# Attention scores of a head pair as two 64-row matmuls instead of stacked 128-row ones

## What is computed

```python
q  = (ln @ Wq).reshape(b, m, h, d).transpose(0, 2, 1, 3)
kv = concatenate([xn @ Wkv, ln @ Wkv], axis=1)        # context rows and token rows
qn = rmsnorm(q, qn_g) * d ** -0.5
kn = rmsnorm(k, kn_g)
sim  = einsum('bhid,bhjd->bhij', qn, kn)              # the scores
attn = softmax(sim, axis=-1)
out  = einsum('bhij,bhjd->bhid', attn, v) @ Wout + bout
```

## Time and profile before

| what | value |
|---|---|
| runs of the kernel before | 2625.65, 2631.70, 2632.07 us |
| span of the profiled execution | 2631.3 us, on its one core |
| mean granted TensorE clock over the span | 0.981 of full |
| TensorE matmuls busy | 2504.6 us, 95% of the span |
| TensorE weight loads busy | 2050.5 us, 78% |
| VectorE, ScalarE, GpSimd busy | 1856.0, 1692.0 and 1309.6 us |
| first and last score matmul start | 93.9 and 1804.3 us |

### The profile page before, as it was taken

One profiled execution on the slowest core, in us unless ns is written; L12 is line 12 of the kernel. 1 busy time (PEld: TensorE's weight loads), 2 busy tenths in 40 slices (PEclk: granted clock), 3 DMA queues, 4 the chain that ended last, 5 costly groups with the idle time before them and its releaser, 6 DMA issues. The chain is left out here.

```text
span 2631.3 us, 45112 instructions
## 1 busy us (share of the span) xinstructions
PE 2504.6 (95%) x14568; PEld 2050.5 (78%) x14568; DVE 1856.0 (71%) x2516; ACT 1692.0 (64%) x2286; POOL 1309.6 (50%) x783
## 2 busy tenths in 40 slices
PE   3799999999999999999999999987989999999998
PEld 3677777777777777777777777755989999999997
DVE  7677777777767767777777776765876557676775
ACT  2578777777777877777777777764332334444443
POOL 4445544454445444554445444531543526666665
PEclk8899999999999999999999999998999999999999
DMA  5845565556646565456645665564841449999996
GB/s 187 242 129 143 166 164 150 134 165 168 167 126 170 150 171 144 134 166 166 156 134 162 167 163 134 134 163 99 174 111 59 139 156 320 322 318 320 326 320 175
DMA packets 258066, 466.63 MB, mean 177 GB/s; under 512 B 65704, under 2 KB 145884, under 8 KB 254025
## 3 DMA queue, kind: packets, MB, share of 16 engines
q1 hardware_dynamic: 231318, 406.54, 54.9%
q0 software_dynamic: 25696, 58.82, 8.3%
q10 hardware_dynamic: 978, 0.34, 0.1%
HBM read 280.90 MB, written 79.85 MB: 137 GB/s over the span
## 5 line engine op out<-in xcount | busy, mean ns | idle before, releaser
L726 DVE TENSOR_TENSOR pr_lo<-pr,pr_hi 128x1024 fp32r<-128x1024 f32 x576 | 816.9, 1427 | 380.8 <-ACT pr_hi L840 376.3
L839 ACT ACTIVATE pr<-ps_s 128x1024 f32<-128x1024 f32 x512 | 526.1, 1028 | 331.0 <-PE ps_s L958 317.6
L840 ACT ACTIVATE pr_hi<-ps_s 128x1024 fp32r<-128x1024 f32 x512 | 522.1, 1020 | 0.0
L972 PE MATMUL ps_o<-pr_hi,vA 128*65 128x512 f32 x1152 | 465.3, 404 | 25.7 <-DVE pr_lo L726 13.3
L464 POOL TENSOR_TENSOR sq<-raw 128x1024 f32<-128x1024 f32 (+1 forms) x96 | 183.3, 1910 | 577.2 <-ACT raw L783 577.2
L974 PE MATMUL ps_o<-pr_lo,vA 128*65 128x512 f32 x1152 | 455.5, 395 | 0.0
L973 PE MATMUL ps_o<-pr_hi,vC 128*65 128x512 f32 x1152 | 453.9, 394 | 0.0
L1605 ACT ACTIVATE ht<-f_ps_h,b 128x256 f32<-128x256 f32 x440 | 184.6, 471 | 342.1 <-PE f_ps_h L1537 342.0
L466 POOL TENSOR_TENSOR rs<-ss,minus_half 128x16 f32<-128x16 f32 (+1 forms) x96 | 261.9, 2728 | 232.8 <-DVE ss L701 232.8
L958 PE MATMUL ps_s<-qq_hi,kk 128*128 128x512 f32 x1152 | 362.7, 396 | 5.7 <-DMA kk<-k_lo 5.3
L958 PE MATMUL ps_s<-qq_lo,kk 128*128 128x512 f32 x1152 | 361.7, 395 | 0.0
(11 more groups left out here) (215 smaller groups left out, 3787.1 us busy)
## 6 DMA issues: line engine op xcount, KB each, us to landing
w<-w1S_dram SPq DMA_DIRECT2D x160, 512.0 KB, 6.0
lnT_sb<-lnT_dram SPq DMA_DIRECT2D x31, 2304.0 KB, 8.8
w2raw<-in_L_ffn_Wproj SPq DMA_DIRECT2D x78, 512.0 KB, 6.8
qq_hi<-q_hi SPq DMA_DIRECT2D x128, 256.0 KB, 5.7
qq_lo<-q_lo SPq DMA_DIRECT2D x128, 256.0 KB, 5.8
kk<-k_hi SPq DMA_DIRECT2D x64, 288.0 KB, 5.9
kk<-k_lo SPq DMA_DIRECT2D x64, 288.0 KB, 5.9
w1S_dram<-cut POOLq DMA_DIRECT2D x36, 512.0 KB, 4.3
```

The source lines that it names most:

```text
L726: v.tensor_tensor(pr_lo[:, d % RING, :], pr[:, d % 2, :], pr_hi[:, d % RING, :].bitcast(F32), ALU.subtract).then_inc(s_lo, 1)
L839: act.activation(pr[:, d % 2, :], ps_s[:, d % 2, :], ACT.Exp, bias=bias)
L840: act.activation(pr_hi[:, d % RING, :], ps_s[:, d % 2, :], ACT.Exp, bias=bias).then_inc(s_exp, 1)
L972: mm(out, upper, pr_hi[:, r, cols], start=k == 0, stop=False)
```

## The change

- The stacked tiles `kk`, `qq_hi`, `qq_lo`, their twelve DMAs a window and the semaphores `s_kq` with all their waits are gone. `k_hi`, `k_lo`, `q_hi`, `q_lo` get two slots, and `turned` writes the slot of the next window.
- A unit is now of both heads of the pair, with one block of 512 queries (g = d // 9). `scores` makes three products, k_hi x q_hi, k_hi x q_lo, k_lo x q_hi, each as one matmul for each head: rows 0 to 63 for head 0, rows 64 to 127 for head 1, into two different PSUM banks. That is six 64-row matmuls in the order head 0, head 1, head 0, and so on.
- `values` makes the same six matmuls a unit, three for each head in place of three for each block of queries. `output`, `spread`, `broadcast` and `store` go by block of queries for both heads; a store writes the same amount to two heads.
- TensorE waits for `s_tlo` once a window, in d = 0.
- Buffers: a tile `fourth` for the prepared operands of the last batch element, which lay in the stacked tiles; `project_out` takes its second `a_hi`, `a_lo` and its `bo` from tiles that are held anyway.

```diff
-        self.k_hi, self.k_lo = t.sb("k_hi", [P, KEYS], F32R), t.sb("k_lo", [P, KEYS], F32R)
-        self.q_hi, self.q_lo = t.sb("q_hi", [P, N], F32R), t.sb("q_lo", [P, N], F32R)
+        self.k_hi, self.k_lo = t.sb("k_hi", [P, 2, KEYS], F32R), t.sb("k_lo", [P, 2, KEYS], F32R)
+        self.q_hi, self.q_lo = t.sb("q_hi", [P, 2, N], F32R), t.sb("q_lo", [P, 2, N], F32R)
...
-        kk = t.sb("kk", [P, 2, 2, KEYS], F32R)
-        qq_hi = t.sb("qq_hi", [P, 2, 2, N], F32R)
-        qq_lo = t.sb("qq_lo", [P, 2, 2, N], F32R)
+        fourth = t.sb("fourth", [P, 2, C, KEYS], F32R)
...
-                if w.turn:
-                    wait_then(s_scores, w.n(UNITS))
-                    wait_then(s_tlo, w.n(TURNS, TURNS + 4))
-                    for h in range(2):
-                        half = slice(DH * h, DH * h + DH)
-                        for part in range(2):
-                            for dst, src in ((qq_hi, q_hi), (qq_lo, q_lo)):
-                                sp.dma_start(dst[DH * part:DH * part + DH, w.other, h, :].bitcast(F32),
-                                             src[half, :].bitcast(F32)).then_inc(s_kq[h], 16)
-                        if h == 0:
-                            wait_then(s_tlo, w.n(TURNS, 2 * TURNS))
-                        for part, src in enumerate((k_hi, k_lo)):
-                            sp.dma_start(kk[DH * part:DH * part + DH, w.other, h, :].bitcast(F32),
-                                         src[half, :].bitcast(F32)).then_inc(s_kq[h], 16)
...
-                if i == 0:
-                    for h in range(2):
-                        wait(act, s_kq[h], w.n(6 * 16, 6 * 16))
...
-                key = kk[:, w.slot, h, k * P:(k + 1) * P]
-                for x, stop in ((qq_hi, False), (qq_lo, True)):
-                    for g in range(QB):
-                        ins = mm(ps_s[:, d % 2, 512 * g:512 * g + 512], key, x[:, w.slot, h, 512 * g:512 * g + 512],
-                                 start=not general and not stop, stop=stop)
+                keys, cols = slice(k * P, (k + 1) * P), slice(512 * g, 512 * g + 512)
+                for i, (key, x) in enumerate(((k_hi, q_hi), (k_hi, q_lo), (k_lo, q_hi))):
+                    for h in range(2):
+                        rows = slice(DH * h, DH * h + DH)
+                        ins = mm(ps_s[:, d % 2, 512 * h:512 * h + 512], key[rows, w.slot, keys], x[rows, w.slot, cols],
+                                 start=not general and i == 0, stop=i == 2)
...
-                            if d % KT == 0:
-                                pe.wait_ge(s_kq[d // KT], w.n(6 * 16, 6 * 16))
+                            if d == 0:
+                                pe.wait_ge(s_tlo, w.n(TURNS, TURNS))
```

More of the change, by code:

```diff
@@ L248, in prepared @@
             if b == B - 1:
-                spare = kk[:, 1, c, :] if part == 0 else (qq_hi, qq_lo)[c][:, 1, :, :].rearrange("p h n -> p (h n)")
-                return spare[:, 0:KEYS]
+                return fourth[:, part, c]
             ring = (pr_hi, pr_lo)[part]
@@ L291, in wait_then @@
                 sp.sem_inc(s_turn, 1)
[L293 to L299, removed]
@@ L819, in upper @@
                     act.wait_ge(c_a0, 32)
-                    for i in range(2):
-                        act.wait_ge(s_kq[i], 6 * 16 * WINDOWS)
-                    act.activation(carry.a_hi[n - 3], carry.a[0][:, h, :], ACT.Copy).then_inc(c_hi, 1)
+                    act.activation(carry.a_hi[0][n - 3], carry.a[0][:, h, :], ACT.Copy).then_inc(c_hi, 1)
             def window(w):
@@ L932, in project, with maximum @@
                 ins.then_inc(s_job, 1)
-            def maximum(w, h):
+            def maximum(w, g):
                 for j in range(NT):
+                    h, tile = j // 4, 4 * g + j % 4
                     if j == 0:
-                        wait(pe, s_exp, w.n(UNITS, KT * h))
-                        if h == 0:
+                        wait(pe, s_exp, w.n(UNITS, KT * g))
+                        if g == 0:
                             pe.wait_ge(s_mask[w.slot], w.v * 32 + 32)
                     else:
[L941 to L945, removed]
+                        pe.wait_ge(s_red, w.n(2 * NT + 2, g * (NT + 1) + j))
+                    rows = slice(DH * h, DH * h + DH)
+                    q = q_hi[rows, w.slot, tile * P:(tile + 1) * P]
+                    for i in range(2):
+                        mm(ps_s[:, 0, 512 * i:512 * i + 512], q, k_hi[rows, w.slot, 512 * i:512 * i + 512], start=True, stop=True)
+                    mm(ps_s[:, 1, 0:P], q, k_hi[rows, w.slot, N:KEYS], start=True, stop=False)
@@ L955, in scores @@
-                key = kk[:, w.slot, h, k * P:(k + 1) * P]
-                for x, stop in ((qq_hi, False), (qq_lo, True)):
-                    for g in range(QB):
-                        ins = mm(ps_s[:, d % 2, 512 * g:512 * g + 512], key, x[:, w.slot, h, 512 * g:512 * g + 512],
-                                 start=not general and not stop, stop=stop)
+                    for h in range(2):
+                        mm(ps_s[:, d % 2, 512 * h:512 * h + 512], ones[:, :],
+                           shift[:, 4 * h:4 * h + 4, :].rearrange("p t q -> p (t q)"), start=True, stop=False)
@@ L964, in values @@
                 slot, d_ = (w.slot, d) if d >= 0 else (w.other, d + UNITS)
-                h, k, r = d_ // KT, d_ % KT, d_ % RING
+                g, k, r = d_ // KT, d_ % KT, d_ % RING
                 pe.wait_ge(s_lo, w.n(UNITS, d + 1))
-                upper, lower = vA[:, slot, k, h, 0:DH + 1], vC[:, slot, k, h, 0:DH + 1]
-                for q in range(QB):
+                for h in range(2):
                     if k == 0:
-                        wait(pe, s_o, w.n(4, 2 * h + q - 1))
-                    cols, out, last = slice(512 * q, 512 * q + 512), ps_o[0:DH + 1, q, :], k == KT - 1
+                        wait(pe, s_o, w.n(4, 2 * g + h - 1))
+                    upper, lower = vA[:, slot, k, h, 0:DH + 1], vC[:, slot, k, h, 0:DH + 1]
+                    cols, out, last = slice(512 * h, 512 * h + 512), ps_o[0:DH + 1, h, :], k == KT - 1
                     mm(out, upper, pr_hi[:, r, cols], start=k == 0, stop=False)
@@ L974, in values @@
                     ins = mm(out, upper, pr_lo[:, r, cols], start=False, stop=last)
-                    if last and q == 0:
+                    if last and h == 0:
                         ins.then_inc(s_pv0, 1)
```

57 lines of the change are left out of this document (30 added, 27 removed).

## The result

| | kernel before | changed kernel |
|---|---|---|
| median of four runs each | 2631.36 us | 2676.62 us |
| lowest and highest | 2625.65 to 2632.07 us | 2675.41 to 2680.75 us |
| span of the profiled execution | 2631.3 us | 2675.3 us |

The ratio is 1.0168, with a 95% interval from 1.0145 to 1.0191: the change makes the kernel 1.7% slower. 2571 us was forecast; the time lies in the range given with it (2515 to 2868 us), on the other side of no change. (The fourth run of the kernel before gave 2631.01 us.)

A forecast was written before the change was run, and what follows sets the result against it. The prediction took TensorE's matmul starts to bound the attention. From 2631.3 us it summed -58 (scores), 0 (row-count changes), -5 (copies) and +3 (output-copy wait) to 2571 us, with a range of 2515 to 2868 us.

The forecast's parts named there:

- TensorE's starts as the clock of the stage: Attention: time is the number of matmuls times the distance of their starts, 0.232 us each for 512 columns.
- Step 1: Scores: six 64-row matmuls for four 128-row ones, 0.83 us against 0.93, -0.10 us a unit, -58 us.
- Step 2: Change between 128-row and 64-row matmuls, twice a unit around the scores: taken as 0, the softest number.
- the case of small borders: Around the scores: heads side by side, each row-count change costing 0.02 to 0.10 us; 2594 to 2686 us, chance 0.15.
- The rival of the drain: Around the scores: each row-count change empties the array, 0.16 us; 2761 us, or 2868 with unhidden loads; chance 0.24.
- Step 3: Twelve copies a window out: TensorE's wait ahead of the first window goes, -5 us, 0 at worst.
- Step 6: What is late next: TensorE's d = 2 wait for VectorE's output copy grows by 0.10 us, +3 us.

The follow-up runs named there:

- e2_same_rows: The changed kernel with both heads' 64-row score matmuls on rows 0 to 63, all else alike: 3054.0 us.
- e3_full_rows: The changed kernel with three 128-row score matmuls a unit in place of the three 64-row pairs (scores not the reference's): 2546.3 us.

## Why the prediction was wrong, point by point

- *TensorE's starts as the clock of the stage:* right before and after. 31 windows, the distance of starts and two ends account for the 44 us.
- *Step 1, side by side:* right that they do, by the rows. Wrong in how: the loads were put one behind the other, 0.119 us apart, from an order seen only where all rows are in use. Loads of different rows run together, two in 0.18 us, and a pair costs one stream; on the same rows they do not (e2_same_rows). The scores from first start to end are 0.33 + 0.24 + 0.23 = 0.80 us, near the 0.83 forecast, but for another reason: 0.10 of it is the first load behind the border.
- *Step 2, the border at 0:* this is the step that failed. It was bounded from 0 to 0.16 us, and the value was taken from a transpose, which changes the form but not the row count. Measured: 0.09 us a border, and the unhidden load, which stood in the rival alone: 0.34 us a plain unit. The text said that 0.05 us a border undoes step 1; it was nearly twice that. The whole sign hung on this number, and the case of small borders, which holds the result (2594 to 2686 us), had a chance of only 0.15. That its range holds the result is luck: with 0.09 us a border the forecast's own sum gives 2571 + 2 x 0.09 x 576 = 2675 us, but by two errors that nearly cancel: the scores 0.13 us a unit too dear (0.83 for three streams) and the loads of 0.16 us left out.
- *The rival of the drain* had both parts of the border, the stall and the unhidden load, but the stall at nearly twice its size: 0.09 us was measured, not the 0.16 us to the recorded end of the matmul before. Its loads (0.19 us a unit) measured 0.16.
- *Step 3:* -5 us forecast, -4.8 found. That VectorE's reciprocals were off the path was a misreading: the 11.9 us in two waits for `pr_lo` of the earlier trace rows lie behind them, in the last window.
- *Step 6:* a wait for the output copy 0.10 us longer was forecast. It went away, because the copy came sooner. Before, it did not start when the last values ended: VectorE first waited for GpSimd's squares (in each of 32 windows), and the copy started at 958.82, 1.43 us after the last values matmul (957.39). In the changed kernel it started 0.52 us after it (987.75), and TensorE needed it at 989.38. Where the unit is shorter the wait was longer, up to 1.2 us (e3_full_rows). Why the squares were in time no run isolates.

```profile
958.30 0.29 DVE L699 TENSOR_REDUCE ss<-sq 128x2 f32<-128x128 f32 x1 [0.29 <-POOL sq L464]
958.82 0.69 DVE L655 COPY o_second<-ps_o 65x512 f32<-65x512 f32 x1
```

```profile
988.27 0.69 DVE L638 COPY o_second<-ps_o 65x512 f32<-65x512 f32 x1
```

- *Not foreseen:* the 11 us in the last window. No run isolates why the sums came back sooner there; no copy of the change is issued in that window. The wait goes with the change: it is 12.7 us in the kernel before with late casts too, and under 7 us in every kernel built on the changed one. The cause stays open.

The Trainium skill, "TensorEngine Tiling (Array Packing)" (Key Properties), says that a change of tiling mode drains TensorE: the traces agree that TensorE stalls there, by 0.09 us and a load (whether the array is empty no row shows), and e2_same_rows shows that it is the row count, not the use of a second tile. The Trainium skill, "TensorE: Matmul & The Clock Gate" (Part 3), says that row tiles start some 4 ns apart and that a load overlaps running matmuls when its row group differs: the starts agree (0.01 us or less). The loads do more than that inside a group of one row count: two of different rows take 0.18 us together, and a load runs beside a matmul on its own rows too (980.61, beside the pair of 980.51). Both were quoted ahead of the run; the sum went by neither.

## What to carry to other kernels

Half-height matmuls of two heads run fully side by side, so they are worth one stream for each pair; but each change of row count costs a stall and an unhidden load, 0.15 to 0.19 us here. A group of them must save more than its two changes cost, about one and a half streams. Here a group of three pairs in place of four matmuls lost 45 us, and a group of six in place of eight won 25 us over the kernel before, 54 us with VectorE's casts out of the way (10 of them the casts' own). Where the sign of a forecast hangs on a price that no row shows, the break-even price belongs in the chances, not only in the text.

## What the runs showed of the hardware

- Two 64-row matmuls on different rows, into different banks: started within 0.01 us, 0.23 to 0.24 us a pair of 512 columns. On the same rows: 0.47 us (e2_same_rows).
- Two 64-row loads of 128 columns on different rows: 0.18 to 0.19 us together, as long as one. On the same rows: 0.41 us (e2_same_rows).
- Between 64 and 128 rows, either way: 0.09 to 0.10 us beyond the stream, after 512 or 384 columns alike. The first load behind it isn't hidden: 0.10 us for 128 columns, 0.07 where it is that of a transpose, 0.06 for 65 columns.
